# Where GpSimd splits weights, and where VectorE normalises batch zero, around the last feed forward of a two-layer transformer kernel

## The reference

```
h = layernorm(x) * (1 + ca) + sa;  x = x + ga * attention(h)
h = layernorm(x) * (1 + cb) + sb;  x = x + gb * feed_forward(h)
```

```
scores = softmax(h @ gate_w.T + gate_b);  top_v, top_i = top_k(scores, 2)
for e in range(8):
    gate  = (top_i == e).sum(-1) * top_v.sum(-1)
    inter = h @ wi.T + bi + (h @ lora_A[e].T) @ lora_B[e].T
    out  += gate * (relu(inter) @ wo.T + bo)
```

## Time and profile before

| | |
|---|---|
| median of 3 runs | 948.13 us (948.01 to 949.83) |
| profiled execution | 956.01 us |
| its span, first to last instruction | 954.3 us |
| PE busy | 902.3 us, 95% |
| ACT busy | 642.4 us, 67% |
| DVE busy | 588.0 us, 62% |
| POOL busy | 306.5 us, 32% |
| mean granted clock of PE | 0.974 |

### The profile page before, as it was taken

How to read it: one execution, slowest core, us unless ns; L and a number is a source line. 1 busy time by engine, 2 the same in 40 slices (tenths; PEclk the granted TensorE clock), 3 DMA queues, 4 the chain that set the end, 5 groups by cost and what they waited for, 6 DMA issues and landing times. The chain is left out here.

```text
span 954.3 us, 25417 instructions
## 1 busy us (share of the span) xinstructions
PE 902.3 (95%) x10209; PEld 665.0 (70%) x10209; DVE 588.0 (62%) x1348; ACT 642.4 (67%) x1094; POOL 306.5 (32%) x393
## 2 busy tenths in 40 slices
PE   8997994599999999999999999999999999998898
PEld 5685773376777776767777776767677776776677
DVE  6556112675666666666666666666666666676895
ACT  3551341487788777878787878887878778874244
POOL 5133803524423233241423333242322324115310
PEclk9998898799999999999999999999999999999899
DMA  8400621000020001002000200200020010000001
GB/s 240 155 2 23 213 88 53 26 1 2 2 92 2 3 25 70 2 2 93 1 3 1 93 2 2 92 2 2 2 92 2 2 33 10 3 1 2 1 12 34
DMA packets 27128, 35.48 MB, mean 37 GB/s; under 512 B 6042, under 2 KB 21716, under 8 KB 26836
## 3 DMA queue, kind: packets, MB, share of 16 engines
q1 hardware_dynamic: 25988, 31.76, 10.2%
q0 software_dynamic: 1024, 2.10, 0.7%
HBM read 28.48 MB, written 5.37 MB: 35 GB/s over the span
## 5 line engine op out<-in xcount | busy, mean ns | idle before, releaser
L566 DVE CUSTOM_DVE_ANT_0 soft<-SC,strips 128x1024 f32<-128x1024 f32 x256 | 303.3, 1222 | 78.3 <-PE SC L407 77.4
L527 ACT ACTIVATE soft<-soft,nmax 128x1024 f32<-128x1024 f32 x256 | 294.2, 1150 | 6.5 <-DVE nmax L566 6.5
L444 PE MATMUL CX<-PTs,V 128*64 128x256 f32 x2048 | 245.1, 381 | 0.0
L512 ACT COPY PTs<-PT 128x1024 f32<-128x1024 f32 x128 | 129.6, 1012 | 135.7 <-PE PT L427 135.7
L407 PE MATMUL SC<-qk 64*128 64x512 f32 x1536 | 210.8, 406 | 3.3 <-DVE nmax L566 1.8
L427 PEld LDWEIGHTS PT<-ident,soft 64*128 64x128 f32 x4096 | 159.6, 140 | 72.0 <-issue 32.5
L444 PEld LDWEIGHTS CX<-PTs,V 128*64 128x64 f32 x2048 | 143.0, 137 | 93.0 <-issue 35.5
L574 DVE COPY PTs<-PT 128x512 f32<-128x512 f32 x128 | 88.5, 692 | 164.5 <-PE PT L427 164.5
L427 PE MATMUL PT<-ident,soft 64*128 64x64 f32 x4096 | 177.1, 226 | 5.7 <-ACT soft L527 3.0
L407 PEld LDWEIGHTS SC<-qk 64*128 64x128 f32 x1536 | 136.7, 187 | 27.2 <-issue 2.1
L607 POOL TENSOR_TENSOR x<-x,wo_out 128x256 f32<-128x256 f32 x64 | 47.1, 736 | 209.3 <-DVE wo_out L583 209.3
(11 more groups left out here) (280 smaller groups left out, 999.8 us busy)
## 6 DMA issues: line engine op xcount, KB each, us to landing
strips<-bias_vec SPq DMA_DIRECT2D x8, 1920.0 KB, 8.3
arena<-in_L_ffn_w SPq DMA_DIRECT2D x1, 2048.0 KB, 12.4
slots_in<-arena SPq DMA_DIRECT2D x1, 1536.0 KB, 8.6
arena<-slots_in SPq DMA_DIRECT2D x8, 192.0 KB, 3.7
slots_out<-arena SPq DMA_DIRECT2D x8, 192.0 KB, 2.0
x<-in_L_attn_x SPq DMA_DIRECT2D x2, 512.0 KB, 4.3
out<-x SPq DMA_DIRECT2D x4, 256.0 KB, 2.3
arena<-in_L_wmod SPq DMA_DIRECT2D x2, 384.0 KB, 5.4
```

The costliest lines, as they stand in the source:

```text
L444: ins = pe.matmul(CX[hd * DK:(hd + 1) * DK, 0:2 * P], V1[:, vb, t, hd * DK:(hd + 1) * DK], PTs[:, g % 2, hd, t, :], start=(t == 0), stop=( ...
L512: act.copy(turned_out(n, 0), turned_in(0)).then_inc(ev("ptA_out"), 1)
L527: act.activation(soft[:, n % RING, hd, :], soft[:, n % RING, hd, :], ACT.Exp, bias=nmax[:, j:j + 1], scale=-1.0, accum_out=rsum[:, hd, n % ...
L566: dve.tensor_tensor_reduce(soft[:, n % RING, hd, :], SC[hd][:, :], strips[:, u // B % 2, hd, i * P:i * P + S], 1.0, 3.4e38, ALU.add, ALU.m ...
```

## The change

- `split_weights` takes one weight at a time. wi is split after POOL's slot 122 (it waits for `wT_ready` 1), lora_B after slot 126, where it was, but now behind a wait for `h_ready` 14, that is, for batch zero's rows on DVE.
- `gate_weights` moves from after slot 129 to after slot 123, with a wait for `wT_ready` 3.
- `split_rows(1)` moves from after slot 129 to after the loop, that is, behind `pool_add(63)` of slot 131.
- On DVE, batch zero's rows move from after slot 125 into slot 126: behind the biased scores of tile 127 and the reciprocal, ahead of `dve_turned(126)`. The instructions are the same eight.
- PE waits for one split weight ahead of `base(0)` and for the second ahead of `lora(0, 0)`.

No instruction that computes is added or removed, and no DMA.

```diff
@@ dve_slot @@
+            if n == TILES - 2:
+                dve.wait_ge(ev("inverse_ready"), 3)
+                for t in range(TB):
+                    ins = dve.tensor_scalar(h[:, t, :], x[:, t, :], mv[:, t, 0:1], st[:, 5, t:t + 1], ALU.subtract, ALU.mult)
+                    if t % 4 == 3:
+                        ins.then_inc(ev("h_ready"), 1)
             if 0 <= n < TILES:
                 dve_turned(dve, n)
@@ gpsimd @@
-            def split_weights():
-
-                pool.wait_ge(ev("wT_ready"), 4)
-                for w, at in enumerate((WI, LB)):
-                    full = wT[:, at:at + FC, :].rearrange("p c d -> p (c d)")
-                    link(pool.tensor_copy(w_parts[:, w, 0, :], full))
-                    pool.tensor_tensor(w_parts[:, w, 1, :], full, w_parts[:, w, 0, :].bitcast(F32),
-                                       ALU.subtract).then_inc(ev("ffn_w_split"), 1)
+            def split_weights(w):
+
+                pool.wait_ge(ev("wT_ready"), (1, 4)[w])
+                full = wT[:, (WI, LB)[w]:(WI, LB)[w] + FC, :].rearrange("p c d -> p (c d)")
+                link(pool.tensor_copy(w_parts[:, w, 0, :], full))
+                pool.tensor_tensor(w_parts[:, w, 1, :], full, w_parts[:, w, 0, :].bitcast(F32),
+                                   ALU.subtract).then_inc(ev("ffn_w_split"), 1)
             def gate_weights():
 
+                pool.wait_ge(ev("wT_ready"), 3)
                 for b in range(B):
...
             for n in range(-2, TILES + 4):
                 pool_slot(pool, n)
+                if n == TILES - 6:
+                    split_weights(0)
+                if n == TILES - 5:
+                    gate_weights()
                 if n == TILES - 4:
                     pool.wait_ge(ev("var_ready"), batches_until(3, 0))
                     inverse_roots(tiles(0))
                 if n == TILES - 2:
-                    split_weights()
+                    pool.wait_ge(ev("h_ready"), 14)
+                    split_weights(1)
                 if n == TILES - 1:
                     split_rows(0)
-                if n == TILES + 1:
-                    split_rows(1)
-                    gate_weights()
-            for k in range(2, 4):
+            for k in range(1, 4):
                 split_rows(k)
@@ vector, after its slot @@
-                if n == TILES - 3:
-                    dve.wait_ge(ev("inverse_ready"), 3)
-                    rows_out(tiles(0))
@@ tensor @@
-            pe.wait_ge(ev("ffn_w_split"), 2)
+            pe.wait_ge(ev("ffn_w_split"), 1)
             base(0)
...
             pe_slot(pe, TILES + 2)
+            pe.wait_ge(ev("ffn_w_split"), 2)
             lora(0, 0)
```

## The result

The changed kernel took 941.28 us, median of 4 runs (939.95 to 943.0), the kernel before in the same comparison 948.07: ratio 0.9918, 95% interval 0.9893 to 0.9943. Faster, by 6.8 us, where 10.5 were forecast; 941.28 lies inside the range given. Two later comparisons of the same pair, with more runs on each side, gave 0.9904 (0.9873 to 0.9934; 941.07 against 952.18) and 0.9904 (0.9878 to 0.993; 941.84 against 950.14), that is, 9.1 us by either ratio (11.1 and 8.3 us by the medians).

The account below looks back on a forecast made before the run. PE, busy 95% of the span, was taken as the bound, losing time idle behind late DVE or at low clock. -4.1, -0.9, -3.3, -3.1, +0.9 = -10.5 us off the 948.13 median gave 937.6, range 934.5 to 943.0.

Parts of the forecast that it names:

- Part one: Batch zero's rows on DVE: with tile 127's biased scores taken first, `pe_turn` of tile 127 starts 4.1 us earlier.
- Clock to the output product, -0.9: PE from tile 127's turn to the output product: 7.6 us at the high clock in place of 8.5.
- rival (a): Rival, chance 0.18: clock still falls, `lora` to the rows' end takes 20.0 us, not 17.9; 8.3 us gained, 939.8 us.
- signs of being wrong: Longer `bn_stats` or biased scores, `masks(0)` waiting over 2 us, low window 868 to 900, PE waiting for splits.
- Part two: Router's steps on DVE: with GpSimd's work elsewhere they cost 3.92 plus 0.4 us, `masks(0)` without idle; 3.3 us saved.
- Part three: `lora(0, 0)` to `turn_rows(3, 3)`: high clock in `lora` saves 3.1 us, hidden sums beside POOL's split cost 0.9.
- Edits costed at nothing: POOL's work moved into the main loop, and the new waits: taken as 0 us, bounds 0 and 5.2.
- From the profile to the median: The 10.5 us worked out on the profiled 956.01 us execution, taken whole off the 948.13 us median: 937.6.
- (b): Rival, chance 0.07: POOL's moved work holds DVE in the main loop, costing 5.2 us; gain 5.3, time 942.8 us.
- (d): Rival, chance 0.04: slower; clock falls within 868 to 884 and stays low; low through 872 to 912 gives 954.8 us.
- (e): Rival, chance 0.06: another releaser, ACT or POOL, stands ready behind DVE at 868 and 884; gain under 1.9, 947 us.
- (c): Rival, chance 0.07: no hidden sums held, no cost of POOL's add beside the router; gain 11.8, time 936.3 us.

Follow-up runs that it names:

- tuned: Changed kernel with POOL's splits of quarters one and three put where DVE reads PSUM: 949.38 us, ratio 0.9893; run again 941.35 us, 0.9914.
- after_again: The changed kernel run again without any edit, in set three, against the kernel before: 941.84 us, ratio 0.9904.

## Why the prediction was right in kind and off in size

The tail shrank by 9.3 us where the sum said 10.5. At `turn_rows(3, 3)` it was 9.2 us, and that stayed to the end, as forecast. Times below are after the scores of tile 127.

- **Part one.** Rows at 4.06 us (said: 4.0), 2.11 long (2.14), `pe_turn` of tile 127 at 6.87 (7.0). Right. But the part is headed by DVE's order, and that is the smaller edit: POOL's part alone has all but 1.5 us of waiting, DVE's order alone 2.3 with POOL still beside the rows.
- **Clock to the output product, -0.9.** This step failed. The output product's end came 1.5 us later than in the working, since the values of group 63 ran at 1.2 GHz. I had taken "no gap of PE above 0.6 us" for "no low stretch". All three profiles of the changed kernel have one low stretch in the tail: at 12.3 us in two of them, where the sixteen router products of 8 columns have just ended and PE had no gap, and at 912.7 in the third, 1.1 us after the wait of 1.85 us, which I had called harmless on one execution's word. In `after_again`, where it fell elsewhere, `lora(0, 0)` starts at 22.40, and the working said 22.49. So the mechanism and the other durations up to there were right to 0.1 us in all, and 1.6 us is the size of what was left out. It is the price of one low stretch, less than rival (a)'s 2.2. Of the signs of being wrong, this one came: a low window between 868 and 900.
- **Part two.** Router's steps 4.16 us (3.92 + 0.4 = 4.32), `masks(0)` without idle. The two experiments that put POOL's work back show the cause. That both router and rows are read as one case, "both work in SBUF", is too coarse: see the last section.
- **Part three.** `lora` 5.69 us (5.55). The hidden sums were held by 0.4 us and not 0.9: `tuned` has 2.73 where the changed kernel has 3.14. The first sum had its relu at 886.18, and POOL's split ended at 887.0 (885.67 + 1.30); only that part of the split could count, the rest fell into a wait that was there anyway. By the Trainium skill's rule on two SBUF inputs (SBUF — State Buffer, "Who interferes with whom") the sums are held beside the split, and so are the router's steps; the traces agree on both.
- **Edits costed at nothing.** Right. DVE's `bn_stats` and biased scores beside the moved work kept their times: all 256 biased scores 1211 to 1226 ns, against 1215 to 1227, and `bn_stats` 0.86 us for four beside the gating (before: 0.86).

```profile
L566 DVE CUSTOM_DVE_ANT_0 soft<-SC,strips x256: 1211/1222/1226, 183.0 to 860.5; 128x1024 f32<-128x1024 f32 x128
```

- **From the profile to the median.** The sum was made against one execution with 10.2 us of low clock in its tail. In the second profile of before there were 6.8, and the tail was 90.7 long; against that the gain is 7.2. The forecast took the 10.5 off the median as if the median execution had the profiled tail; its reason was only that no difference was known. The 7.2 lies within the first comparison's interval (5.4 to 10.1 us). How much low clock the unprofiled executions had in their tails is not known, so this last step is an estimate.

Rivals: (a) came true in a milder form and at another place; (b), (d) and (e) did not occur. Of (c), half of the sums' hold was absent. That the time lies inside the range owes something to its width: the 937.6 itself was 3.7 us low.

## What to carry to other kernels

When DVE work on the path is several times longer than the same instructions elsewhere in the trace, look at what GpSimd does beside it, and move GpSimd's work to where DVE reads PSUM: it cost nothing in the attention loop, where DVE had biased scores, copies out of PSUM and `bn_stats`, and 3 us beside the router. That DVE reads only one tensor from SBUF is not enough. The normalised rows (x and two numbers per row) do so and took 5.94 us in place of 2.14; the spread copies do so and took 1.73 in place of 0.76 beside two adds. Test such a move separately from the reorder that comes with it; here the move was three quarters of the waiting saved. Before costing a stage from one profile, find out how much low clock that execution had, and compare idle time of the bounding engine, not only spans.

## What the runs showed of the hardware

- TensorE's granted clock fell to 0.50 for 3.4 us without any gap of PE ahead of it, right at the end of sixteen router products of 8 columns. Ten profiles have the changed kernel's order of PE up to there (the changed kernel three times and seven variants); in five the stretch begins 12.2 to 12.6 us after the scores of tile 127, in five it is absent. With DVE's part alone a low stretch also began right behind these products (872.2; they ended at 871.9). What decides stays open.
- Executions of one kernel differ by 6 us with it: before at 946.8 to 947.7 us has a mean clock of 0.980, at 950.9 to 953.4 of 0.973 to 0.977.
- POOL's products in SBUF lengthened single DVE steps with two SBUF inputs from 0.22 to as much as 1.18 us, and a DVE reduction beside them not at all (0.22, L1265 and L1268 in the gating's timeline). Instructions with one tensor from SBUF differ: `rows_out` and the spread copies grew (above), four `bn_stats` took 0.86 us both beside the gating and alone.
